# Three depthwise convolutions on aligned row pairs, with 64x64 quarters in groups in place of some whole blocks

## The reference, cut to what matters

```
q, ctx, gates = y[..., :C], y[..., C:2*C], y[..., 2*C:]
ctx_all = 0
for l, k in enumerate((k0, k1, k2)):              # depthwise 3x3, 5x5, 7x7
    ctx = gelu(dwconv_same(ctx, k))
    ctx_all = ctx_all + ctx * gates[..., l:l + 1]
ctx_global = gelu(mean of ctx over the image)
ctx_all = ctx_all + ctx_global * gates[..., 3:]
```

## Time and profile before

| | |
|---|---|
| median of 3 runs | 9431.66 us |
| lowest and highest | 9427.26 and 9441.87 us |
| span of the profiled execution, first to last instruction | 9428.0 us |
| that execution's own time around its span | not given by the page |
| PE, DVE, POOL, ACT busy | 89%, 68%, 60%, 48% of the span |
| convolution stage: first to last of its large matmuls | 4547.8 to 6303.2 us |
| focal input stage, from its first odd pair copy to its last | 3930.3 to 4514.2 us |

### The profile page before, as it was taken

The page is one execution under the profiler, slowest core; times in us unless marked ns, Lnnn a source line. Parts: engine busy times, 40 slices in busy tenths (PEclk is TensorE's granted clock), DMA queues, the critical chain, the costliest instruction groups (busy, mean ns, idle before and its releaser), DMA issues. The chain is left out here.

```text
span 9428.0 us, 326077 instructions
## 1 busy us (share of the span) xinstructions
PE 8402.8 (89%) x109727; PEld 5286.7 (56%) x109727; DVE 6370.0 (68%) x21703; ACT 4557.5 (48%) x12677; POOL 5660.4 (60%) x6830
## 2 busy tenths in 40 slices
PE   7999999798888998688899999978888888888888
PEld 6777777644444443466455555547776745555554
DVE  8999999799999998688355555547777722222222
ACT  5666666555555555588333333324444433333333
POOL 8999999788888887677122222215555544444444
PEclk9999999899999999899999999988898989999999
DMA  1222222111111111489444444437777712222222
GB/s 53 58 58 58 58 58 58 54 56 54 51 55 54 53 55 58 136 269 275 171 148 168 151 147 169 151 113 177 169 170 169 158 50 56 56 57 56 56 56 54
DMA packets 798423, 960.01 MB, mean 102 GB/s; under 512 B 323868, under 2 KB 662593, under 8 KB 774352
## 3 DMA queue, kind: packets, MB, share of 16 engines
q1 hardware_dynamic: 798032, 956.25, 35.5%
HBM read 576.90 MB, written 455.45 MB: 109 GB/s over the span
## 5 line engine op out<-in xcount | busy, mean ns | idle before, releaser
L966 PE MATMUL moe_pe_out<-moe_we,moe_xnT 128*128 128x512 f32 x3136 | 1531.1, 622 | 227.8 <-DVE moe_acc L860 218.5
L1571 PE MATMUL conv_pc<-conv_c,conv_toep 128*128 128x432 f32 (+1 forms) x3584 | 1371.1, 535 | 0.0
L762 ACT ACTIVATE moe_scaled<-moe_pe_out,moe_gate 128x128 f32<-128x128 f32 x3136 | 892.4, 368 | 791.6 <-PE moe_pe_out L966 789.9
L2133 ACT ACTIVATE rec_yT<-rec_ph 128x32 f32<-128x32 f32 x3136 | 618.3, 197 | 1241.5 <-PE rec_ph L2254 1241.5
L1433 POOL TENSOR_TENSOR conv_g<-conv_c,conv_gate 128x896 f32<-128x896 f32 x128 | 365.6, 2856 | 1410.9 <-DVE conv_out L1534 1370.9
L966 PEld LDWEIGHTS moe_pe_out<-moe_we,moe_xnT 128*128 128x128 f32 x3136 | 560.2, 195 | 1026.7 <-issue 1020.1
L282 POOL TENSOR_SCALAR att_xn<-att_xin,att_mv,att_rstd 128x128 f32<-128x128 f32 x1024 | 1006.7, 996 | 54.2 <-POOL att_rstd L278 54.2
L2254 PE MATMUL rec_ph<-rec_yT,rec_vt 128*32 128x32 f32 x25080 | 843.6, 207 | 196.3 <-ACT rec_yT L2133 121.7
L1571 PEld LDWEIGHTS conv_pc<-conv_c,conv_toep 128*128 128x128 f32 x3584 | 671.9, 190 | 602.4 <-issue 602.4
L2180 DVE COPY rec_xT<-rec_pin 128x512 f32<-128x512 f32 x196 | 135.6, 692 | 1240.6 <-PE rec_pin L2226 1240.6
L2254 PEld LDWEIGHTS rec_ph<-rec_yT,rec_vt 128*32 128x32 f32 x25080 | 494.6, 108 | 648.9 <-ACT rec_yT L2133 609.8
(11 more groups left out here) (202 smaller groups left out, 20292.9 us busy)
## 6 DMA issues: line engine op xcount, KB each, us to landing
conv_toep<-rows_dram SPq DMA_DIRECT2D x32, 2304.0 KB, 14.0
c<-foc_cs SPq DMA_DIRECT2D x32, 1856.0 KB, 15.5
conv_cin<-c SPq DMA_DIRECT2D x32, 1856.0 KB, 9.0
ctx_all<-conv_out SPq DMA_DIRECT2D x32, 1792.0 KB, 6.5
att_xin<-x_windows SPq DMA_DIRECT2D x512, 98.0 KB
x<-att_x1s SPq DMA_DIRECT2D x1024, 49.0 KB
moe_xin<-x SPq DMA_DIRECT2D x112, 448.0 KB, 3.5
x<-moe_acc SPq DMA_DIRECT2D x112, 448.0 KB, 2.7
```

Of the source, the lines that this page charges most:

```text
L762: ins = act.activation(scaled[:, b, e, :], pe_out[:, b, 1, e * C:(e + 1) * C], ACT.Identity, scale=g)
L966: pe.matmul(pe_out[:, b, half, :], xnT[:, n.slot(2), t, :], we[:, half * 4:half * 4 + 4, :].rearrange("d e c -> d (e c)"), start=True, sto ...
L1571: ins = pe.matmul(pc[k][:, half, 0:HALF * wide].rearrange("p (b i) -> p b i", i=wide)[:, :, i0:i1], w, tile[:, b, i0 + away:i1 + away], st ...
L2133: act.activation(yT[:, a, cs], ph[:, a, cs], ACT.Sigmoid).then_inc(moved, 1)
```

## The change

Row pairs now start at the first real row: r = 1 + 2j, so 28 pairs (`EVEN`) hold 56 rows. The odd pair, its two matmuls and two activations are gone from the focal input stage, and `c0`, `cs`, `gs` and `cin` have 28 pairs for 29. The gates go out in one DMA for two.

In the convolution stage input and output of all three convolutions have the same alignment. A block is named by how many pairs away its input is. The centre (away 0) is a full 128 x 128 matmul in all three, and so are the two neighbours (away 1 and -1) of the third. What lies outside is done in quarters of 64 x 64 of the banded matrix: (HIGH, LOW) means input partitions 64 to 127 and output partitions 0 to 63. The first convolution needs two quarters at distance 1, the third two at distance 2, the second four in its two neighbours at distance 1 that keep their half (LOW, LOW and HIGH, HIGH) and two that cross. `four` issues two crossing quarters of the first or third convolution with two of the second, `crossed` the last two of the second. A new semaphore `corners_made` orders the second convolution's quarters. The third GELU has two activations of 128 partitions. On ACT and PE the end of the second convolution moves behind the third.

```diff
-ODD = IMG // 2 + 1
@@ focal input, PE
-                for i, j0, jn in pair_groups(c):
...
-                        r = 2 * (j0 + j)
+                for j in range(GRP):
+                    r = 1 + 2 * (GRP * c + j)
@@ focal input, SP
-                for half, j0 in ((0, 0), (1, 1)):
-                    sp.dma_start(dram(gates, m.val(EVEN, half * ROW * 4 * B * EVEN), [(4 * B * EVEN, ROW), (B * EVEN, 4), (1, EVEN)]),
-                                 gs[(1 - half) * ROW:(2 - half) * ROW, s, :, j0:j0 + EVEN]).then_inc(g_out[s], 16)
+                sp.dma_start(dram(gates, m.val(EVEN), [(4 * B * EVEN, P), (B * EVEN, 4), (1, EVEN)]),
+                             gs[:, s, :, :]).then_inc(g_out[s], 16)
@@ convolution, ACT
-                    for row in range(2):
-                        at, to = (1 - row) * ROW, row * ROW
-                        ins = act.activation(dst[to:to + ROW, n.slot(slots), b, :], pairs[at:at + ROW, :, row:row + EVEN],
-                                             ACT.Gelu, scale=gap[at:at + ROW, :])
+                for half in range(2):
+                    ins = act.activation(c3[:, n.slot(2), images(half), :], image_pairs(pc[2], half), ACT.Gelu, scale=gap[:])
+                ins.then_inc(activated[2], 1)
...
                 if last < -3:
-                    gelu(0, n + 2, first + 2)
-                if last < -2:
-                    gelu(1, n + 1, first + 1)
+                    gelu1(n + 2, first + 2)
                 if first >= 1:
                     average(n - 1, first - 1)
                 if last < -1:
-                    gelu(2, n, first)
+                    gelu3(n, first)
+                if last < -2:
+                    gelu2(n + 1, first + 1)
@@ convolution, PE
+            LOW, HIGH, ALL = (0, ROW), (ROW, P), (0, P)
+            def block_of(k, n, half, away, rows=ALL, outs=ALL, start=False):
+                g = Step(n.loop, U // PER, n.off // PER)
+                s, ch = g.slot(2), n.off % PER
+                tile = (cin[:, s, :, ch, :], c1[:, n.slot(4), :, :], c2[:, n.slot(2), :, :])[k]
+                at = T_OFF[k] + FURTHEST[k] - P * away
+                (r0, r1), (m0, m1) = rows, outs
+                i0, i1 = max(0, -away), min(EVEN, EVEN - away)
+                w = toep[r0:r1, s, ch, at + m0:at + m1]
+                return pe.matmul(image_pairs(pc[k], half)[m0:m1, :, i0:i1], w,
+                                 tile[r0:r1, images(half), i0 + away:i1 + away], start=start, stop=(rows != ALL), skip_group_check=True)
+            def crossed(k, n, half, far):
+                block_of(k, n, half, -far, HIGH, LOW)
+                return block_of(k, n, half, far, LOW, HIGH)
+            def four(across, half, low, high, n):
+                k, m, far = across
+                block_of(k, m, half, -far, HIGH, LOW)
+                block_of(1, n, half, low, LOW, LOW)
+                second = block_of(1, n, half, high, HIGH, HIGH)
+                first = block_of(k, m, half, far, LOW, HIGH)
+                return first, second
...
+                if has1:
+                    centre(0, n + 2, first + 2)
+                if has2:
+                    centre(1, n + 1, first + 1)
+                if has1:
+                    four((0, n + 2, 1), 0, -1, 1, n + 1)
+                    made1, made2 = four((0, n + 2, 1), 1, -1, 1, n + 1)
+                    made1.then_inc(convolved[0], 1)
+                    made2.then_inc(corners_made, 1)
...
+                if has3:
+                    centre(2, n, first)
                 if first >= 1:
                     average(n - 1, first - 1)
-                if last < -1:
-                    convolve(2, n, first, 0)
+                if has3:
+                    beside(n)
+                if has2:
+                    _, made2 = four((2, n, 2), 0, 1, -1, n + 1)
+                    made2.then_inc(corners_made, 1)
+                    made3, made2 = four((2, n, 2), 1, 1, -1, n + 1)
+                    made3.then_inc(convolved[2], 1)
+                    hold(pe, corners_made, n.val(3, 2), ticks)
+                    made2.then_inc(corners_made, 1)
+                    crossed(1, n + 1, 0, 1)
+                    hold(pe, corners_made, n.val(3, 3), ticks)
+                    crossed(1, n + 1, 1, 1).then_inc(convolved[1], 1)
```

More of the change, by code:

```diff
@@ L1288, in context @@
                 m, c = image(n)
[L1289 to L1297 removed]
+                if first >= 2:
+                    hold(pe, c_read, n.val(1, -1), ticks)
+                    hold(pe, g_read, n.val(1, -1), ticks)
+                for j in range(GRP):
+                    r = 1 + 2 * (GRP * c + j)
+                    ins = pe.matmul(py[:, n.slot(2), j, 0:C + 4], xnT[:, m.slot(2), r:r + 2, :].rearrange("p r w -> p (r w)"),
+                                    wf[:, C:OUT], start=True, stop=True)
+                ins.then_inc(c_made, 1)
             def step(n, first, last):
@@ L1377, in convolution_stage, with images, image_pairs @@
         NG = N // PER
+        def images(half):
+            return slice(half * HALF, (half + 1) * HALF)
+        def image_pairs(bank, half):
+            return bank[:, half, 0:HALF * EVEN].rearrange("p (b i) -> p b i", i=EVEN)
         @block.sync
@@ new lines, in gelu1, with gelu2 @@
+                    act.wait_ge(gated1, n.val(1, -3))
+                    act.sem_inc(ticks, 1)
+                    act.wait_ge(convolved[1], n.val(1, -3))
+                for half in range(2):
+                    ins = act.activation(c1[:, n.slot(4), images(half), :], image_pairs(pc[0], half), ACT.Gelu, scale=gap[:])
+                ins.then_inc(activated[0], 1)
+            def gelu2(n, first):
+                act.wait_ge(convolved[1], n.val(1, 1))
+                if first >= 2:
+                    act.sem_inc(ticks, 1)
+                    act.wait_ge(gated2, n.val(1, -1))
+                    act.sem_inc(ticks, 1)
+                    act.wait_ge(convolved[2], n.val(1, -1))
+                for half in range(2):
+                    ins = act.activation(c2[:, n.slot(2), images(half), :], image_pairs(pc[1], half), ACT.Gelu, scale=gap[:])
+                ins.then_inc(activated[1], 1)
@@ new lines, in gelu3 @@
+            def gelu3(n, first):
+                act.wait_ge(convolved[2], n.val(1, 1))
+                if first >= 2:
+                    act.sem_inc(ticks, 1)
+                    act.wait_ge(gated3, n.val(1, -1))
+                    act.sem_inc(ticks, 1)
+                    act.wait_ge(pooled_part, n.val(1, -1))
+                for half in range(2):
+                    ins = act.activation(c3[:, n.slot(2), images(half), :], image_pairs(pc[2], half), ACT.Gelu, scale=gap[:])
+                ins.then_inc(activated[2], 1)
```

118 lines of the change are left out of this document (55 added, 63 removed).

## The result

The changed kernel takes 9300.81 us (median of 4 runs, 9293.7 to 9306.38), where the kernel before takes 9431.42 (4 runs). The ratio is 0.9854, 95% interval 0.984 to 0.9868. The forecast was 9303, in a range of 9235 to 9400. The profiled execution took 9298.81 us, its span is 9297.0, so 131.0 less than before.

A forecast was written before the change was run, and what follows sets the result against it. PE's streamed passes bound the convolution stage; loading ends last in focal input. From 9428.0, minus 119 (0.95 us by about 125 steps), 1 at the stage's end and 8 focal, gives 9300 span, forecast 9303, range 9235 to 9400.

The forecast's parts named there:

- Quarters of a group stream together: Convolution stage: four quarters stream at once, six groups taking 4.35 us a channel, where serial quarters would take 14.5.
- Rival 1: Convolution groups: row tiles of one PSUM bank take turns, 4.35 us more a channel, 9848 in all; chance 0.07.
- Rival 2: Convolution quarters: passes start strictly in program order, 7.25 us for 4.35 a channel, 9667 in all; chance 0.04.
- Changes between array and tiles: Convolution on PE: switching to tiles and back costs 0.32 us a pair, 0.64 a channel; bounds nothing and 1.4.
- Rival 3: Convolution: array and tile changes cost their upper bound, 1.4 us a channel, ACT late by 0.2; 9421; chance 0.03.
- (a): Second convolution's centre needs its bank read by ACT; it fits with 0.1 us to spare, 0.03 put on it.
- (b): Third convolution: ACT's two activations end at 1.53 us, free before the next pair; all that six for eight buys.
- (c): Two holds on PE's own corner quarters, each covered by a group of 0.72 us streaming; they cost nothing.
- (d): Convolution: DVE, seven operations of 1.07 us each, ends at 7.1, the third activation at 7.9: 0.8 us spare.
- The 8 us for the lighter queue: Focal input stage: smaller context store, 64 KB of 5.1 MB an image, 0.25 us; saving taken as 8, bounds 0 and 50.
- taken alone: Focal input stage: removing the odd pair's waits, taken alone, is about 1.7 us an image, 29 to 31 times, 50 us.
- Rival 4: Focal input stage tightens too: loads are issued earlier and 40 us more come, 9260 in all; chance 0.06.

The follow-up runs named there:

- the written-out ones: Focal input loop written out step by step with four image buffers: changed kernel with one phase of quarters 9246.96 us, kernel before the change 9478.47 us.

## Why the prediction was right, and where it was not

*Quarters of a group stream together.* Right: first passes within 0.02 us, second ones 0.41 later, the next group's first 0.36 after those; the run on one tile prices the opposite at 1138 us over the kernel before. Both traces of tiles that the forecast went by, with 49 and 128 columns, held for 432. Rival 1, row tiles of one bank taking turns, would have put the time at 9848; crossed quarters, two row tiles writing to different partitions of one bank, start within 0.02 us (5416.18 and 5416.20, second passes 0.36 later). Rival 2, passes strictly in order, would have given 9667; the four starts at 5408.30 to 5408.32, ahead of the earliest second pass at 5408.71, disagree.

*Changes between array and tiles.* Forecast 0.32 a pair. In the trace: into tiles 0.09 of gap and 0.05 in the first pass, back 0.09 and 0.10, 0.33; by the three kernels with one to three pairs 0.36 to 0.38. With two pairs a channel's sum is 11.98 + 0.66 = 12.64, measured 12.65. The forecast's 12.65 was made of 0.64 and 0.03 for ACT; the first was 0.02 too little by the trace (0.08 to 0.12 by the three kernels), the second not there. Taking 0.33 a pair off the three distances leaves 11.96, 11.99 and 12.04, so some 0.03 to 0.05 us a pair lie outside these gaps; they were not located. Rival 3's 1.4 us a channel is out.

*Waits.* (a) ACT's pair for the second convolution holds back the weights by 0.44 and the matmuls by nothing. (b) ACT free in time: right, and more is in it than the forecast said. It called this all that six activations for eight buy. The run with eight lost 1.21 us a channel, more than the gain of 0.95. (c) The holds cost nothing where a group streams beside them; 0.31 where none does. (d) DVE kept its slack: it still waits 1.07 us a channel for the third activation (126.6 us, 118 times, from 4600 to 6100).

*Convolution stage.* The forecast had 125 full steps by 0.95, 119, and 1 us at the end; the stage is 125.5 shorter. There are 124 full steps between averages, and they give 118.4. The last three, in which less and less is left to compute, give 4.4, and what lies ahead of the first average 2.7: this part was mis-sized by 6.

*Focal input stage.* This term failed. "Loading is already what ends last, so what the odd pair gives PE and DVE is handed to the wait for the load" was right in its first half. In both kernels DVE first reads nearly every image of the loop 0.4 us after its load has landed. DVE's named waits for the load went from 15.2 us to

```profile
  DVE foc_stat L1205: 25.3, 14
```

which is 10 us more, not all of what the odd pair took. The 8 us for the lighter queue were mis-sized: images are 19.2 us apart, 19.1 before. From 3940 to 4480 a load lands 12.5 to 14.2 us after its issue, 13.3 in the median in both kernels, and the next one is issued 5.5 us after the image is first read; 13.3 + 0.4 + 5.5 is the distance of the images. So it is the time of that one transfer, not the bytes of all queues, that the loop waits for: with four buffers the distance fell to 17.2 us, with the DMA engines 92% busy between two turns. That nothing of the 1.2 us an image of the odd pair came through is shown by the pair of kernels with four buffers, and by that of the written-out ones (42.9 us); the forecast's "taken alone" was 1.7 us an image. Rival 4, which had these us come through, did not happen.

*Granted clock.* The forecast said 1.00 throughout. It is 1.00 in the convolution stage, but from 3940 to 4480 it is 0.97, where it was 1.00 before: in ten short stretches, nine of 3.4 us and one of 6.8, it is 0.50. No run separates what they cost.

The forecast of 9303 came out at 9301, closer than its terms. Against it the convolution stage is 5.5 us shorter and the focal input stage 9.5 longer; the four stages whose code did not change do the rest, modulation and recurrent 11.0 shorter, attention and experts 4.1 longer. That these leave 3 us is luck. The mechanism stands on the 12.65 us a channel.

## What to carry to other kernels

Small tiles paid here because four of them streamed at once, at 0.36 us a pass for the whole group, as for one full block; on one tile the same quarters put the averages 22.70 us apart, not 12.65. A pair of changes between whole array and tiles cost 0.36 to 0.38 us, so do them in as few phases as the buffers allow. When an engine that is idle two thirds of the time gets one more piece (ACT here, at 1.21 us a channel), look at who stands behind it, not at its share. When work is taken from a stage and the stage does not get shorter, lift what ends last (here the buffers of the load), and then look at single rounds of the loop: their mean hid a stall of 8 us that came at every turn.

## What the runs showed of the hardware

- A loop's turn cost 9 to 10 us when its body had grown from two images to four, 8.1 of them idle, with instruction transfers in every turn; straight code had at least as many transfers (58 from 3940 to 4435, against 50 up to 4480) and no stall. Another loop, unchanged, cost 5 us more a turn (79.5 against 74.5) when code ahead of it had grown. Loops over other numbers of images were not tried.
- PE fed four tiles at once from a program in which the tiles' first matmuls are two apart (first passes 13 ns apart, 5402.42 to 5402.46).
- Two quarters with different rows of the array and different output partitions of one PSUM bank stream side by side (crossed quarters, starts within 0.02 us at 5416.18 and 5416.20, 0.36 us a pass for the group).
- The attention stage has two lengths, about 1833 and 1877 us, with the same code. The cause stays open.
